# A graph network kernel: edge records made piece by piece in f16 with gathers over 128 partitions, and one-hots built per half pair in planes

## The reference

```python
x = _layernorm(x + L0(x))   # agg = segment_sum(x[src], dst); relu((x + agg) @ W1 + b1) @ W2 + b2 + x @ Wres + bres
x = _layernorm(x + L1(x))   # twice: (h + mean over the edges of h) @ Wa.T, @ Wb.T, relu
x = _layernorm(x + L2(x))   # 4 steps: neigh = sum of norm * h[src]; xc + 0.1 * tanh(xc @ A.T + neigh + bias)
x = _layernorm(x + L3(x))   # relu(segment_sum(x[src] @ W + b + edge_attr_6 @ We + be, dst))
```

## Time and profile before

| | us |
|---|---|
| median of 3 runs | 1170.55 (1166.4 to 1171.84) |
| the profiled execution | 1174.38, of which span 1172.6 |
| setup, until the first one-hot of the build | 90.1 |
| pairs 0 and 1 of the build | 90.1 to 136.8 |
| pairs 2 to 12 | 136.8 to 311 |
| layer 0 and rounds | 319 to 1172.6 |

### The profile page before, as it was taken

How to read it: one execution, slowest core, us unless ns; L and a number is a source line. 1 busy time by engine, 2 the same in 40 slices (tenths; PEclk the granted TensorE clock), 3 DMA queues, 4 the chain that set the end, 5 groups by cost and what they waited for, 6 DMA issues and landing times.

```text
span 1172.6 us, 25349 instructions
## 1 busy us (share of the span) xinstructions
PE 1045.7 (89%) x10553; PEld 640.1 (55%) x10553; DVE 534.5 (46%) x1036; ACT 288.3 (25%) x590; POOL 69.4 (6%) x69
## 2 busy tenths in 40 slices
PE   0245788889879999999999999999999999999997
PEld 0234677777655565555546555475544755447455
DVE  4397699999452335632222213232231313544333
ACT  0246688888561000000000000000000001212100
POOL 3811000000000000000000000000000000000000
PEclk9855799999989999999999999999999999999999
DMA  5404566777789586587766987669865798745941
GB/s 187 106 13 110 215 280 284 290 327 309 293 328 377 198 327 238 228 324 294 274 227 235 371 344 257 226 251 373 343 254 209 275 378 315 266 169 202 411 154 31
DMA packets 60761, 301.78 MB, mean 257 GB/s; under 512 B 12026, under 2 KB 15210, under 8 KB 57125
## 3 DMA queue, kind: packets, MB, share of 16 engines
q1 hardware_dynamic: 49768, 290.54, 64.6%
q0 software_dynamic: 8416, 9.50, 3.0%
q10 hardware_dynamic: 2522, 0.98, 0.4%
HBM read 235.69 MB, written 65.26 MB: 257 GB/s over the span
## 4 chain that ended last, share of the span: by engine, by line
PE 78%; DMA 9%; DVE 5%; issue 3%; ACT 3%; ACTq 2%; DVEq 0%; SPq 0%
PE ps L1253 45%; PE ps L1246 17%; DMA weight_mats<-arena 8%; PE ps L1208 4%; PE ps L1364 3%; PE ps L1339 3%; PE ps L1163 2%; PE ps L1221 2%; ACTq L956 1%; DVE arena L676 1%; DMA edge_table<-arena 1%; ACT arena L1012 1%; ACTq L959 1%; ACT x_buf L1067 1%; PE ps L1190 0%
## 5 line engine op out<-in xcount | busy, mean ns | idle before, releaser
L1253 PE MATMUL ps<-arena,parts_even 125*128 125x500 f32 (+2 forms) x700 | 267.5, 537 | 0.0
L1253 PE MATMUL ps<-arena 125*128 125x500 f32 (+2 forms) x700 | 267.5, 537 | 0.0
L1253 PEld LDWEIGHTS ps<-arena,parts_even 125*128 125x128 f32 x700 | 129.4, 188 | 120.6 <-issue 106.7
L1253 PEld LDWEIGHTS ps<-arena 125*128 125x128 f32 x700 | 129.3, 188 | 120.5 <-issue 106.7
L996 ACT ACTIVATE XT<-ps 128x500 f32<-128x500 f32 (+2 forms) x49 | 26.5, 540 | 492.3 <-PE ps L1221 492.3
L1246 PE MATMUL ps<-arena 125*128 125x500 f16 (+3 forms) x700 | 140.6, 354 | 1.7 <-DVE arena L708 1.3
L1364 PE MATMUL ps<-arena 64*128 64x52 f16 (+1 forms) x6500 | 106.7, 181 | 38.9 <-DVE arena L676 23.6
L1010 ACT ACTIVATE arena<-ps 128x400 f16<-128x400 f32 (+1 forms) x195 | 125.0, 641 | 42.4 <-PE ps L1364 36.1
L1364 PEld LDWEIGHTS ps<-arena 64*128 64x128 f16 x6500 | 96.7, 96 | 56.8 <-ACT arena L1012 31.7
L1012 ACT ACTIVATE arena<-ps 128x400 f32<-128x400 f32 (+1 forms) x195 | 117.7, 604 | 0.0
L671 DVE TENSOR_TENSOR arena<-arena 128x4224 f16<-128x4224 f16 (+2 forms) x52 | 116.2, 2235 | 0.0
(11 more groups left out here) (184 smaller groups left out, 721.1 us busy)
## 6 DMA issues: line engine op xcount, KB each, us to landing
arena<-weight_mats SPq DMA_DIRECT2D x20, 3250.0 KB, 11.9
arena<-weight_mats SPq DMA_DIRECT2D x20, 3000.0 KB, 11.9
arena<-count_mats SPq DMA_DIRECT2D x15, 3125.0 KB, 14.3
weight_mats<-arena SPq DMA_DIRECT2D x13, 3125.0 KB, 14.6
count_mats<-arena SPq DMA_DIRECT2D x13, 1562.5 KB, 6.2
arena<-weight_mats SPq DMA_DIRECT2D x4, 2437.5 KB, 8.9
arena<-weight_mats SPq DMA_DIRECT2D x4, 2250.0 KB, 8.5
arena<-count_mats SPq DMA_DIRECT2D x3, 2343.8 KB, 8.6
```

Of the source, the lines that this page charges most:

```text
L1253: ins = t.matmul(o, xs[:, k, :], rhs, start=(k == 0), stop=(k == NC - 1))
```

## The change

Setup:
- The window gather, the pointers, the 25 chunk gathers and the later attribute gathers (`attrs`) cover 128 partitions where they covered 125; x is loaded as 112 and 13 rows. The last three partitions carry nothing that is used.
- Records are written as f16 (`rec`; two f32 buffers `hi32`, `lo32` for the steps between), in six blocks of 3, 3, 5, 5, 5 and 4 chunks (`REC_AT`), each behind its own gathers. A block has ten instructions still: the largest-weight reduce and the f16 copy are gone, the two degree sums are in. The weight check reads the table's weights once, early. On DVE the blocks stand between the other work: 0, 1, check of x, 2, low half of x, 3, weights, 4, a few rows, 5.
- PE transposes the f16 records with an f16 identity, in groups between its other work; the last group uses bank 6. ACT takes over three weight copies and two of the fold, and copies columns group by group. The three loads of `bcol` go from ACT's queue to SP's. The product that spreads `W8`, and its copy, stand ahead of `mode` instead of behind it.

Build: `produce` works by half pair (67 and 58 columns). The low one-hot is one instruction for the half (L694), both weight products another (L698), into three planes; the 128-wide ones stay by step (L687). `hot_lo` is one buffer a half, `hot_hi` still two by step, and each has its own wait on PE's units.

The diff, cut:

```diff
-CG = 5
+REC_AT = (0, 3, 6, 11, 16, 21, NC)
...
-        hot_lo = [at(83704 + 14008 * i, 128, [STEP_MAX, 3 * LO], F16) for i in range(2)]
+        hot_lo = [at(92408 + 10452 * i, 128, [3, HALF_MAX, LO], F16) for i in range(2)]
...
-        win_i = at(20000, NP, [WIN], I32)
+        win_i = at(20000, 128, [WIN], I32)
...
-        sdw = at(51200, NP, [NC, SLOTS, 3])
+        sdw = at(54000, 128, [NC, SLOTS, 3])
...
-        rec = [at(75000 + 6656 * i, NP, [NC + 1, SLOTS]) for i in range(5)]
+        rec = [at(40000 + 3328 * i, NP, [NC + 1, SLOTS], F16) for i in range(4)]
...
-            sp.dma_start(Xn[:, :, :], x.rearrange("(p c) f -> p c f", c=NC)).then_inc(x_in, 16)
+            for a, z in ((0, 112), (112, NP)):
+                sp.dma_start(Xn[a:z, :, :], rows[a:z]).then_inc(x_in, 16)
...
+            def records(i):
+                cs, n = slice(REC_AT[i], REC_AT[i + 1]), REC_AT[i + 1] - REC_AT[i]
+                dve.wait_ge(sd_in[i], 16 * n)
...
+                wait_used(UNITS_TO[u + 1] - UNITS)
+                v.tensor_tensor(eq.rearrange("p t (a j) -> p t a j", j=2), numbers(iota_lo, n, LO),
+                                code(lo_c[:, bass.ds(q, 1), t0:t0 + n, :], LO), ALU.is_equal).then_inc(eq_ok, 1)
+                dve.wait_ge(eq_ok, 2 * q + half + 1)
+                v.tensor_tensor(hot_lo[half][:, 1:3, 0:n, :].rearrange("p k t m -> p t k m"),
+                                eq.unsqueeze(2).to_broadcast([128, n, 2, LO]),
+                                both.unsqueeze(2).to_broadcast([128, 2 * n, LO // 2, 2]), ALU.mult)
+                rows_hot(u).then_inc(hots_ok, 1)
+                rows_hot(u + 1).then_inc(hots_ok, 1)
...
-                                                   hot_lo[b][rows, e, LO * a:LO * z],
+                                                   hot_lo[half][rows, a:z, e_lo, :],
```

More of the change, by code:

```diff
@@ L84, in groups_to, with recs_to @@
     return sum(a < k for a in GROUP_AT[:-1])
+def recs_to(k):
+    return sum(a < k for a in REC_AT[:-1])
 def layer_of(r):
@@ L637, in _ @@
+            records(5)
+            link(v.tensor_reduce(flags[0:NP, 1:2], cntR[:, 0:NC, last], AX, ALU.max))
             v.tensor_reduce(flags[:, 0:1], flags[:, :], AX, ALU.max).then_inc(flag_ok, 1)
-            v.tensor_reduce(S8[:, :, 0], cntR[:, 0:NC, :], AX, ALU.add)
-            link(v.tensor_reduce(S8[:, :, 1], w_slots, AX, ALU.add))
             def degrees():
@@ L677, in produce, with wait_used, rows_hot @@
[L677 removed]
+                def wait_used(unit):
+                    dve.wait_ge(sums_ok, UNITS * q + unit + SUMS_PAD)
+                def rows_hot(u):
+                    wait_used(UNITS_TO[u - 2] - (UNITS if u < 2 else 0))
+                    t0, n = STEP_AT[u], STEP_AT[u + 1] - STEP_AT[u]
+                    return v.tensor_tensor(hot_hi[u % 2][:, 0:n, :].rearrange("p t (a j) -> p t a j", j=2),
+                                           numbers(iota_hi, n, 128), code(hi_c[:, bass.ds(q, 1), t0:t0 + n, :], 128),
+                                           ALU.is_equal)
@@ L862, in fast @@
                 dve.wait_ge(iotas, 1)
+                dve.wait_ge(col_ok, 4)
+                for half in range(2):
+                    produce(0, half)
                 dve.wait_ge(col_ok, 16)
-                dve.wait_ge(w8_ps, 1)
-                link(v.tensor_copy(W8_rep[:, :], ps[:, SUM_BANK, 0:D]))
-                dve.sem_inc(w8_ok, 1)
-                with dve.Fori(0, PAIRS) as q:
-                    for u in range(STEPS):
-                        produce(q, u)
+                with dve.Fori(1, PAIRS) as q:
+                    for half in range(2):
+                        produce(q, half)
                 dve.wait_ge(sq_ok, 1)
@@ L979, in _ @@
                 ins.then_inc(col_ok, 1)
+            for b in range(4):
+                record_columns(b)
+            for i, k in enumerate(WT):
+                if k != "L2_W":
+                    act.wait_ge(wt_ps, len(WT))
+                    s.activation(WT[k][:, :], ps[:, 4, i * D:i * D + D], ACT.Copy).then_inc(wt_copied, 1)
+            for b in range(4, 8):
+                record_columns(b)
+            act.wait_ge(fold_ps, 1)
+            s.activation(L1_W[0][:, :], ps[:, 5, 0:D], ACT.Copy)
+            s.activation(L1_W[1][:, :], ps[:, 5, D:2 * D], ACT.Copy).then_inc(fold_copied, 1)
+            for b in range(8, 16):
+                record_columns(b)
             act.wait_ge(deg_ok, 1)
@@ L1117, in _ @@
                 t.transpose(ps[:, 4, i * D:i * D + D], raw_w[:, RAW.index(k), :], ident[:, :]).then_inc(wt_ps, 1)
+            for b in range(4, 8):
+                record_rows(b)
             pe.wait_ge(wt_copied, 3)
```

274 lines of the change are left out of this document (139 added, 135 removed).

## The result

The changed kernel took **1143.39 us** in the median of 4 runs (1141.16 to 1146.07) beside 1170.43 (1166.4 to 1171.84) for the kernel before: a ratio of 0.977, interval 0.975 to 0.980, 27.0 us less. Predicted were 1145.5 and 1136 to 1159. The profiled execution is one of 1141.16 us with a span of 1139.4.

The account below looks back on a forecast made before the run. TensorE bounds the rounds, two successive chains (POOL's gathers, DVE's records) setup, and stores the build from pair 1. Savings of 21.2 + 1.2 + 1.8 + 0.9 = 25.1 us from 1170.55 give 1145.5, range 1136 to 1159.

Parts of the forecast that it names:

- Windows and table: Start of setup: windows and table store over 16 DMA engines bring the first chunk gather 7.5 us earlier, at 14.6.
- Gathers: Chunk gathers in setup: 1.52 us apart undisturbed, 2.0 us of waits added; the last starts at 56.1 and lands at 59.7.
- Records and `mode`: End of setup: the last record block ends at 63.3 and `mode` is written at 66.3, 21.2 us earlier.
- `mode` to the first one-hot: Start of the build: 1.4 us instead of 2.6, as the `W8` copy moves ahead of `mode`; 1.2 us gained.
- ACT's remaining copies hide: Start of the build: ACT's last 6 us of copies fit under DVE's first 5.3 us of one-hots, or miss by under 1.
- Pair 0: First pair of the build: one-hots in 8 instructions take 14.0 us plus 0.15, where the pair took 15.9; 1.8 us less.
- 26.1 both ways: Second pair of the build: PE's first unit comes 5.3 us after the previous pair's last one-hot before and after the change.
- early clock: Rival, chance 0.16: TensorE's clock rises before pair 1, saving up to 9.7 us more; at half of that, 1140.5 us.
- Steady pairs: Pairs 2 to 12 of the build: the stores' 16.0 us replaces 16.14 a pair, 0.9 us over the nine that count.
- Half rate: Rival, chance 0.05: the weight product in the build slows to 1.09 ns a value, 5.4 us more a pair; 1190.5 us.
- x is no issue: Setup: x lands some 15 us before its use, and ACT makes its high half before record block 2 ends.
- POOL pays: Rival, chance 0.19: the chunk gathers in setup slow by 0.5 us each, 12 us in all; 1157.5 us.

Follow-up runs that it names:

- e1: The kernel before with only the transfers over 128 rows (x as 112 and 13), records and one-hots as before: 1160.16 us, ratio 0.991.
- e7: The changed kernel with TensorE giving its first counts before its wait for all 12 record copies: 1154.30 us.
- e6: The changed kernel with the one-hots of before and TensorE's first counts given before its wait for the record copies: 1156.83 us.
- e3: The changed kernel with the one-hots of before (a step at a time, not in planes): 1158.5 us.
- e5: The changed kernel, unchanged, measured again: 1154.72 us.
- e8: As e7, with 20 unused TensorE products ahead of pair 0 while DVE makes the first one-hots: 1155.64 us.
- e4: The kernel before with only the new one-hots by half pair in planes: 1167.8 us, ratio 0.998.
- e11: The changed kernel with one more VectorE instruction, an unused maximum, in each half of a pair: 1184.56 us.
- e2: The changed kernel with all transfers back over 125 rows: 1156.14 us, ratio 0.988.
- e10: The changed kernel with only the 25 chunk gathers back over 125 rows: 1145.63 us, ratio 0.977.
- e9: As e7, with all six record blocks on DVE ahead of the work that waits for ScalarE: 1146.95 us, ratio 0.977.

## Why the prediction was right, and where it wasn't

The time, 1145.5 for 1143.4, was right, and so was the kind of gain: nearly all of it is in setup. Term by term:

- **Windows and table.** The first gather at 14.72, predicted 14.6, and by the path predicted: DVE takes up the windows at 10.79 (predicted 10.6; the terms given, 6.07 + 2 + 1.5, make 9.6, and the windows were there by 10.2), and the gather starts 3.93 us later, the interval of before. The table store was complete at 14.4 (9.12 + 5.3 of landing), 1.1 us later than predicted. It cost nothing beside pointers written at 13.77, where before POOL started 0.94 us behind the same instruction; e1, whose pointers are there at 13.01, still starts at 14.69, so any faster way to the pointers would meet the store. The share of the DMA engines was as predicted; the rule of the Trainium skill on it ("DMA: Bandwidth & Descriptors", "Why a DMA increments its semaphore by 16 and not by 1") agrees here: landing of the windows fell from 12.0 to 4.5 us, of the table from 9.3 to 5.3.
- **Gathers, the step that failed.** "Undisturbed, POOL issues every 1.52 us: 1.21 of work": over 128 rows it is 0.95 of work and 1.25 between starts, below my lower bound ("as now"). Landing took 2.6 us, not 3.6. The last gather started at 48.4, not 56.1. So DVE is the bound from 25.8 on and not POOL: the last data are there at 51.0, 5.8 us before DVE comes to the last block at 56.8, and not 2 us behind it. The locks came as said, 3.7 us of POOL's time in all (33.7 for 24 intervals of 1.25), but off the path. The gather beside L627 took 3.55 us and ended 0.83 us after it, which agrees with the Trainium skill ("SBUF — State Buffer", "Who interferes with whom").
- **Records and `mode`.** Last record 60.4, predicted 63.3; from it to `mode` 2.2 us, predicted 3.0. `mode` 24.9 us earlier for 21.2.
- **`mode` to the first one-hot.** 2.3 us and not 1.4. "ACT's remaining copies hide" was wrong in a way the order of the code shows: PE gives the count that DVE's first wait needs behind its own wait for ScalarE's twelfth copy. e7 shows the 1.4, and that the time moves by 0.4 us with it, no more than noise.
- **Pair 0.** From first one-hot to store 0 the gain was 0.7 us, predicted 1.8. 1.25 of the 1.8 were the wait for PE of the earlier trace rows, which the sum drops without a reason. The wait is indeed gone and DVE's one-hots take 14.3 us (64.90 to 79.2), as predicted; what failed is that store 0 would follow them, for it now comes 5.6 us behind the last and not 4.6. In the same setup the old one-hots even reach store 0 0.4 to 0.8 us sooner after the `inv_n` store (e6 and e7, e3 and e5): PE's first unit waits for 5.5 us of one-hots instead of 4.1, and ScalarE's copies fill the rest of the pair (e8).
- **Pair 1.** "26.1 both ways" failed: 22.0. Four kernels with the old one-hots have 25.1 to 26.1, and the nine with the new ones and no added work 21.0 to 22.9. In like pairs of kernels (before and e4, e3 and e5, e6 and e7) the new ones are worth 2.6 to 3.3 us there. The rival "early clock" does not explain it. Before pair 1 the clock is at 0.50 in after, and 0.76 at 92 to 96 us is a stretch in which PE was busy for 0.6 of 4 us. The mean granted clock over pair 1 is 0.62 in before and e3 and 0.78 in e1 and e6, all with the old one-hots, for 26.1, 25.3, 25.1 and 25.6 us; with the new ones it is 0.71 to 0.83 for 21.0 to 22.9 us, 0.71 in after. So old and new one-hots differ by some 3 us at the same mean clock, and the old ones alone hardly differ between 0.62 and 0.78. In after DVE is busy for 14.35 us of pair 1 and in before for 15.29, so of the 4.1 us only 0.9 are its work and the rest shorter waits; which wait makes it stays open. e4 puts all of the one-hots at 2.3 us of time, near the 2.7 that I had, from other terms.
- **Steady pairs.** 16.10 for 16.14 and not 16.0: 0.3 us (0.14 over nine pairs would have been 1.3, not the 0.9 in the sum). The stores do pace them (landing unchanged, pairs of every variant at 16.06 to 16.11). "Half rate" is refuted, L698 took 1.97 us; e11 gives its price, some 30 us for 3.3 us a pair.
- **What I didn't see.** "x is no issue: it would land some 15 us before its use." x lands in time, but its way leads through seven copies that wait for PE's counts, and in most later executions three or four of them take 2 to 10 us each. The slow result this gives, 1154.7, lies in my range and near the rival that I had called "POOL pays" (1157.5), but by luck: it is another mechanism, and POOL is undisturbed in it, 0.95 us a gather.

The sum was right in part by luck, because terms missed to both sides: 3.7 us more in setup, 0.9 and 1.1 less at the start of the build, 4.1 more in pair 1, 0.6 less in the steady pairs, 30.3 in all for 25.1. With the 3 us of the rounds, and less the 6.2 of the two executions' places, that is the 27 measured.

By parts, each against before measured beside it: one-hots alone 2.3 us (e4); with records as they land, all over 125 rows, 13.9 (e2); with windows and x over 16 DMA engines 26.7 (e10; the table store, of 128 rows in all kernels, lands sooner with them); and the chunk gathers over 128 rows on top bring 27.0 without stops and 14.3 with them. e10 is the version to keep.

## What to carry to other kernels

Choose the row count of a transfer so that it spreads over all DMA engines where bytes are many (windows and x: 13 us here), and measure it apart from the many small gathers, which gained 2 us at best and in most executions lost 9 or more. Put work that waits for another engine behind all work that doesn't, even where that engine should long be ready: e9 shows stops like e5's and is 8 us faster (11 by the changes). And measure a changed kernel in more than one session: the four runs of the first told of a kernel of 1143 us.
